# A ninth harmonic in half-height matmuls, and feature rows gathered once and doubled by ScalarE, in a four-layer graph kernel

## The reference

```python
h = jnp.maximum(_layernorm(x, axis=-1), 0.0)
q = (h @ Wq).reshape(n, H, DQK)                       # 8 heads of 16
x_dst = h[edge_dst]                                   # one feature row of 64 for each edge
wk = mlp2(edge_features, k_w1, k_b1, k_w2, k_b2)      # edge weights, 128 each
wv = mlp2(edge_features, v_w1, v_b1, v_w2, v_b2)
# tensor_product: out[e,o] = w[e,o] * sum_{s<9, d<64} x_dst[e,d] * sh[e,s] * C[d,s,o]
k = tensor_product(x_dst, edge_sh, wk, Cqk).reshape(-1, H, DQK)
v = tensor_product(x_dst, edge_sh, wv, Cv).reshape(-1, H, DV)
attn = jnp.einsum('ehd,ehd->eh', q[edge_src], k)
# softmax of attn over the edges of a node, weighted sum of v, W_out, W_self, batch norm
```

## Time and profile before

| | us |
|---|---|
| median of three runs | 3084.54 |
| lowest and highest run | 3083.05, 3087.43 |
| the profiled execution | 3079.32 |
| its span, first to last instruction | 3077.6 |
| TensorE busy in the span | 2460.3 (80%) |
| VectorE busy | 2185.3 (71%) |
| GpSimd busy | 2028.1 (66%) |
| ScalarE busy | 869.0 (28%) |

### The profile page before, as it was taken

How to read it: one execution, slowest core, us unless ns; L and a number is a source line. 1 busy time by engine, 2 the same in 40 slices (tenths; PEclk the granted TensorE clock), 3 DMA queues, 4 the chain that set the end, 5 groups by cost and what they waited for, 6 DMA issues and landing times. The chain is left out here.

```text
span 3077.6 us, 51541 instructions
## 1 busy us (share of the span) xinstructions
PE 2460.3 (80%) x14042; PEld 2123.6 (69%) x14042; DVE 2185.3 (71%) x5057; ACT 869.0 (28%) x2421; POOL 2028.1 (66%) x2116
## 2 busy tenths in 40 slices
PE   6777777525676677477777778999999999999997
PEld 5677777525566566355555557888888888888884
DVE  5555555536888888555555564888888888888885
ACT  1111111136666664111111111222232232222233
POOL 4777777457777771177777746777777766677630
PEclk9777767657888888599999987999999999999996
DMA  3444443133333330145555557898888888899850
GB/s 94 93 88 87 86 86 86 32 69 63 60 59 60 61 56 7 29 154 154 162 154 159 158 153 187 213 215 210 206 207 214 205 208 204 204 214 206 205 136 11
DMA packets 334088, 404.37 MB, mean 131 GB/s; under 512 B 171480, under 2 KB 203334, under 8 KB 333898
## 3 DMA queue, kind: packets, MB, share of 16 engines
q1 hardware_dynamic: 252362, 251.19, 35.2%
q0 software_dynamic: 66560, 96.41, 14.8%
q10 hardware_dynamic: 14976, 54.53, 5.2%
HBM read 339.81 MB, written 62.07 MB: 131 GB/s over the span
## 5 line engine op out<-in xcount | busy, mean ns | idle before, releaser
L1941 PE MATMUL psum<-ckv,z 128*128 128x256 f32 x4160 | 967.1, 383 | 0.0
L1941 PEld LDWEIGHTS psum<-ckv,z 128*128 128x128 f32 x4160 | 766.1, 191 | 97.7
L1776 POOL DMA_INDIRECT acc<-QW,dst_i x416 | 398.5, 958 | 183.9 <-issue 111.5
L234 POOL DMA_INDIRECT ga<-TA,src_i x416 | 411.0, 988 | 155.9 <-issue 126.5
L1786 POOL DMA_INDIRECT ga<-XX,src_i x416 | 399.6, 961 | 156.5 <-issue 122.5
L1033 POOL DMA_INDIRECT ga<-T,src_i x416 | 401.4, 965 | 147.2 <-issue 125.9
L234 POOL DMA_INDIRECT ga<-T,src_i x416 | 396.0, 952 | 149.2 <-issue 124.3
L2058 DVE TENSOR_TENSOR z<-psum,shb 128x2560 f32<-128x2560 f32 x104 | 293.2, 2819 | 58.6 <-PE psum L1932 58.3
L1127 PE MATMUL psum<-HT,wy 128*128 128x128 f32 x1664 | 263.4, 323 | 65.7 <-DVE wy L1400 64.9
L451 PE MATMUL psum<-wre,re 128*128 128x68 f32 x832 | 210.9, 345 | 129.4 <-DVE oneT L296 81.7
L1127 PEld LDWEIGHTS psum<-HT,wy 128*128 128x128 f32 x1664 | 241.5, 231 | 83.7 <-DVE wy L1400 77.1
(11 more groups left out here) (366 smaller groups left out, 4199.0 us busy)
## 6 DMA issues: line engine op xcount, KB each, us to landing
shb<-in_ea SPq DMA_DIRECT2D x104, 640.0 KB, 6.9
WKV<-wkvo ACTq DMA_DIRECT2D x104, 512.0 KB
shb<-in_ea SPq DMA_DIRECT2D x104, 512.0 KB, 9.1
wkv<-WKV SPq DMA_DIRECT2D x104, 512.0 KB
dl<-DL SPq DMA_DIRECT2D x208, 128.0 KB
win<-TB SPq DMA_DIRECT2D x416, 32.0 KB
ga<-T,src_i POOLq DMA_INDIRECT x832
ef<-in_ea SPq DMA_DIRECT2D x104, 128.0 KB
```

The costliest lines, as they stand in the source:

```text
L234: pool.indirect_dma_start(o, None, table, bass.IndirectOffsetOnAxis(ap=src_i[:, g * GT + t:g * GT + t + 1], axis=0)).then_inc(s_g[k], 16)
L1776: pool.indirect_dma_start(qg[:, (g % QR) * GT + t, :], None, QW, bass.IndirectOffsetOnAxis(ap=dst_i[:, g * GT + t:g * GT + t + 1], axis=0) ...
L1941: last = pe.matmul(kv_of(k)[:, t, :], z[:, k % 2, j, t * 128:(t + 1) * 128], ckv[:, j, :], start=(j == 0), stop=(j == NZ - 1))
```

## The change

The table `XX` holds each feature row once (256 bytes), stored straight from the normalised rows `H`; the second copy in the node stage is gone. The gathers fill the first 64 columns of a place in `ga`. A new ScalarE step, `second_halves`, waits for the gather of a group and copies the 64 columns to the other 64; it stands at the head of ScalarE's body and works for the group one ahead, and the transposes wait for it (`e3_two`) instead of the gather.

The ninth harmonic is now loaded into both halves: the lower half is used for tiles 0 and 1, the upper for tiles 2 and 3, by a third transfer of 2 x 128 columns per group. The upper half of the last slot of `ckv` holds the ninth constants too. In front of the first tile's products stand four matmuls with 64 rows of contraction, one per tile, in the order 0, 2, 1, 3, so that lower and upper half alternate; they open the accumulation. Each tile then has four products with 128 rows.

```diff
-        XX = dram("XX", [N, 2 * D])
+        XX = dram("XX", [N, D])
-        NL3 = 9
+        NL3 = 11
-        twice = nodes[:, NJ * D:3 * NJ * D].rearrange("p (j a f) -> p j a f", j=NJ, a=2)
-                pool.memset(ckv[D:128, NZ - 1, :], 0.0).then_inc(n3_p, 1)
-                        pool.indirect_dma_start(ga[:, (g % GR) * GT + t, :], None, XX, bass.IndirectOffsetOnAxis(
+                        pool.indirect_dma_start(ga[:, (g % GR) * GT + t, 0:D], None, XX, bass.IndirectOffsetOnAxis(
...
+                    late = bass.ds(g * GT * W + 2 * W, 2 * W)
+                    sp.dma_start(shb[D:128, k % 2, NZ - 1:NZ, 2 * W:], A["ea9"][NS - 1:NS, late].partition_broadcast(D)).then_inc(e3_e[k % 2], 16)
...
+                    L(m[D:128, NZ - 1:NZ, :], A["L3_gnn_" + w][:, NS - 1:NS, :])
...
-                    sp.wait_ge(n3_x, h + 1)
-                    put_rows(sp, XX.rearrange("(p j) f -> p j f", p=PN)[:, J, :], twice[:, J].rearrange("p j a f -> p j (a f)"), n3_ox)
+                    sp.wait_ge(n3_h, h + 1)
+                    put_rows(sp, XX.rearrange("(p j) f -> p j f", p=PN)[:, J, :], H[:, J, :], n3_ox)
...
+                def second_halves(i, k):
+                    act.wait_ge(e3_g[k], i * 64 + 64)
+                    rows = ga[:, (k % GR) * GT:(k % GR + 1) * GT, :]
+                    act.activation(rows[:, :, D:F], rows[:, :, 0:D], ACT.Copy).then_inc(e3_two, 1)
+
                 def body(i, k):
                     p1, p2 = soft_1(i, k), soft_2(i, k)
+                    n = i * UG + k + 1
+                    if n < NT // GT:
+                        second_halves(n // UG, n % UG)
...
-                for h, (J, _) in enumerate(HALVES):
-                    act.wait_ge(n3_h, h + 1)
-                    act.activation(twice[:, J, 1, :], twice[:, J, 0, :], ACT.Copy).then_inc(n3_x, 1)
...
                 act.wait_ge(e3_i, 3)
+                second_halves(0, 0)
                 each_step(act, body)
...
-                    pe.wait_ge(e3_g[k], i * 64 + 64)
+                    pe.wait_ge(e3_two, g + 1)
...
-                    for j in range(NZ):
+                        for u in (0, 2, 1, 3):
+                            half = slice(0, D) if u < 2 else slice(D, 128)
+                            pe.matmul(kv_of(k)[:, u, :], z[half, k % 2, NZ - 1, u * 128:(u + 1) * 128], ckv[half, NZ - 1, :],
+                                      start=(u % 2 == 0), stop=False, skip_group_check=True)
+                    for j in range(NZ - 1):
                         last = pe.matmul(kv_of(k)[:, t, :], z[:, k % 2, j, t * 128:(t + 1) * 128], ckv[:, j, :],
-                                         start=(j == 0), stop=(j == NZ - 1))
+                                         start=False, stop=(j == NZ - 2), skip_group_check=True)
...
-                dve.memset(shb[D:128, :, NZ - 1, :], 0.0).then_inc(e3_pad, 1)
+                dve.memset(shb[D:128, :, NZ - 1, 0:2 * W], 0.0).then_inc(e3_pad, 1)
...
-                    dve.wait_ge(e3_e[k % 2], i * (UG // 2 * 32) + (k // 2 + 1) * 32)
+                    dve.wait_ge(e3_e[k % 2], i * (UG // 2 * 48) + (k // 2 + 1) * 48)
```

More of the change, by code:

```diff
@@ L1713, in build @@
         NODE3 = len(R3) * 5 + 2
-        e3_zero = sem("e3_zero")
+        e3_zero, e3_two = sem("e3_zero"), sem("e3_two")
         e3_gq = [sem(f"e3_gq{k}") for k in range(UG)]
@@ L1980, in node_transposes @@
                     for j in range(n):
-                        last = pe.transpose(bank[r % 2][0:D, j * PN:(j + 1) * PN], twice[:, j0 + j, 0, :], ident[0:PN, 0:PN])
+                        last = pe.transpose(bank[r % 2][0:D, j * PN:(j + 1) * PN], H[:, j0 + j, :], ident[0:PN, 0:PN])
                     last.then_inc(n3_t, 1)
@@ L2007, in _ @@
                 pe.wait_ge(n3_qc, len(R3))
-                pe.wait_ge(n3_p, 1)
                 pe.sem_inc(e3_S, SPARE)
@@ L2040, in _ @@
                 for J, _ in HALVES:
-                    dve.scalar_tensor_tensor(twice[:, J, 0, :], XC[:, J, :], 0.0, st[:, 5, J].unsqueeze(2).to_broadcast([PN, J.stop - J.start, D]),
+                    dve.scalar_tensor_tensor(H[:, J, :], XC[:, J, :], 0.0, st[:, 5, J].unsqueeze(2).to_broadcast([PN, J.stop - J.start, D]),
                                              ALU.max, ALU.mult).then_inc(n3_h, 1)
```

## The result

The changed kernel takes 3068.06 us, the median of 8 runs (3061.38 to 3072.81). The kernel before, run beside it, takes 3083.90 us (8 runs, 3077.94 to 3087.43). The ratio is 0.9945, with a 95% interval of 0.9935 to 0.9955: 0.55% faster. Forecast were 3063 us and a range of 3048 to 3098.

A forecast was written before the change was run, and what follows sets the result against it. TensorE and VectorE were both near their limit, with VectorE's chain the bound afterwards. 28 us gained in groups 11 to 103 less 7 lost at the start gave net -21, 3058 us against the profile, 3063 as median; range 3048 to 3098.

The forecast's parts named there:

- loss at the start: Bodies 6 and 10 of the fourth edge stage: ScalarE waits for a gather ahead of dT; +7.5 us once, bounds +2 and +10.
- overlap of the half products: Front of each group's products: 64-row matmuls on different halves run beside each other, saving three slots, 0.65 us per group.
- change between full and half rows: TensorE, going in and out of the half-row products: 0.2 us charged per group, bounds 0 to 0.29.
- TensorE's net saving: TensorE in each group, products saved less the price of changing row height: 0.45 us.
- TensorE's own work: TensorE's time without waits over a cycle of four groups: 42.73 us before, 40.93 us after the change.
- VectorE's chain: VectorE's own dependent steps over four groups, without waits for TensorE: 41.97 us, unchanged, and setting the period afterwards.
- gain, groups 11 to 103: Steady part of the fourth edge stage: 93 groups at 0.30 us each, 28 us gained.
- before the first transposes: Node stage to first gathers: fewer ScalarE copies and a halved table save 0 to 2 us, a copy costs 0.42; -0.5 taken.
- Who is late next: Steady part: VectorE's 41.97 us stand above TensorE's 40.93 per four groups; VectorE's waits for TensorE go, 0.30 us per group.
- ScalarE's waits for gathers: ScalarE after 2100 us: such waits would show that gathers gate, a rival at 3070 to 3088 us, chance 0.10.
- DMA: DMA engines: shorter gather rows save 0.43 us per group, the new 64 KB cost about 0.3; share up 0.02 or 0.03.
- No overlap: Rival, front of each group's products: 64-row matmuls don't overlap, TensorE is the bound at 43.53 us per cycle; 3098 us, chance 0.19.

## Why the prediction was right, point by point

The sign, the mechanism and the range held; the time is 5 us above the forecast. Two terms of the sum were mis-sized, in opposite directions: the gain was put 8 us too high, the loss at the start 1.4 to 2.7 us too high. That they partly cancel is luck.

| step | predicted | measured |
|---|---|---|
| overlap of the half products, per group | 0.65 us | 0.86 us |
| change between full and half rows | 0.20 us | 0.38 us |
| TensorE's net saving, per plain body | 0.45 us | 0.48 us |
| TensorE's own work, one cycle | 40.93 us | 40.86 us |
| VectorE's chain, one cycle | 41.97 us | 42.21 us, mean 42.32 |
| gain, groups 11 to 103 | 28 us | 19.66 us |
| loss at the start | 7.5 us | 4.83 us at group 11, 6.08 at 15 |
| before the first transposes | -0.5 us | -0.26 us |
| sum | -21 us | -15 us |

**The products.** Two errors cancel, by luck. Four slots are saved, not three: my picture of passes that begin in issue order is wrong. The change of tiling costs 0.09 us ahead of the half products (0.53 us after the transposes start, where full rows followed at 0.44), 1.06 - 4 x 0.216 = 0.20 us with them, and 0.10 us in the eight full products behind (1.83 us to the sums, 8 x 0.216 = 1.73), 0.39 us by this count. I took its price from a single one-row transpose, and the upper bound of 0.29 was too low. The page "TensorEngine Tiling (Array Packing)" of the Trainium skill (Key Properties) says that a change of mode drains TensorE. The trace shows that the change costs time, 0.38 us for both directions; whether it is a drain it doesn't show, since the ends of matmuls in it are modelled.

**Who is late next.** Right, and the experiment without the ninth harmonic shows it, though the cycle of 42.2 to 42.3 us lies above the 41.9 to 42.1 that I had named as the sign. The size of the gain is the step that failed: I put it at all that VectorE waited for TensorE, 1.22 us per cycle. The measured gain is 43.30 - 42.32 = 0.98 us, and the difference of 0.24 is the wait of z for prow. In before this wait is not on the list: z waited 0.49 us for the transposes at the same place, and a wait is put down to what came last. By the order of the program the second one lay under it, half as long. Removing a wait uncovers the next at the same instruction; the chain I worked out without TensorE's waits had to be put together from what each step needs, not by subtraction. Over 92 groups 0.06 us make 5.5 of the 8.3 us. Most of the rest is a wait in body 14 (below).

**The start.** The place and the mechanism are right: gather 7 holds ScalarE, dT comes behind it, and VectorE and TensorE stand. The size was 7.5 at group 11, and came out at 4.83. I had said that by body 14 the lead is large enough. It isn't: at 2028.88 VectorE waits another 2.12 us for dT, and between groups 11 and 15 the loss grows to 6.08 us.

**ScalarE's waits for gathers.** I had named them, after 2100 us, as the sign that gathers gate. They are there: 39.7 us from 2100 to 2900, up to 5.7 us at a time, and harmless, since ScalarE is idle then and nothing behind the wait is late. The sign that tells is VectorE's wait for dT, which is missing after body 14.

**DMA.** I had the new 64 KB at 0.3 us of all 16 engines per group, and a rise of the share by 0.02 or 0.03. It rose by 0.05. With and without that transfer the share is 0.97 and 0.92 at the same cycle of 10.6 us, so it takes 0.5 us. The shorter gather rows give about as much back (0.85 against 0.89 of 10.8 us, 0.43 us, as predicted). I called both zero for the time. For TensorE and VectorE they are; but with 512-byte rows the half products alone scatter up to 3103 us. What the shorter rows are worth is room on the DMA engines, and that I did not see.

**The rivals.** No overlap was put at 3098 us and measures 3124. Its condition was right, its price was not: against before it was put at +14 us and is +35 (3123.62 against 3088.51 beside it). TensorE's own work with overlap is 2 x 9.93 + 10.53 + 10.47 = 40.86 us per cycle. (The first softmax body lasts 11.54 us, and in it L681 starts 1.44 us after the transposes, where in before it was 0.43: 1.01 us are waiting.) Eight slots instead of four add 4 x 0.86 = 3.4, 44.3 in all, where I had 43.53, mostly because the change of tiling costs 0.38 us and not 0.2. The measured 44.65 holds another 0.36 us of waiting for VectorE: L681 starts 0.79 us after the transposes there (2515.58 and 2516.37). The bound from which no overlap would decide, a net saving of 0.16 us per group, doesn't follow from the prediction's own figures either: (42.73 - 41.97) / 4 is 0.19.

## What to carry to other kernels

A list of waits names for each instruction only the one that came last, so a gain that is read from it is an upper bound: look for what the same instruction needs next, and when that is ready. When two engines are within 3% of each other, find out which chain is the bound by taking work from each in turn; here 75 us in 800 less of TensorE's work gave nothing, and two small copies taken from VectorE gave 12 us (3062.62 to 3050.68). A new wait on an idle engine that works in order belongs behind whatever another engine is waiting for, and ahead of anything that itself waits late: against before, the same copy of 0.4 us cost 6 us of the start at the head of the body and 2 us behind dT; at the body's end the kernel got 120 us slower than after, part of it by the lower clock that followed the stall.

## What the runs showed of the hardware

- Two float32 matmuls of 64 rows on different halves start together and follow in pairs every 0.216 us, the pace of one full-row instruction, whether they are issued alternating or one half after the other. On one half they follow one by one at the same pace.
- Going from full rows to 64-row products and back cost 0.38 us in a plain body, spread over three places, and not as a gap at one of them.
- After TensorE had stood 3.6 us in every cycle, its granted clock was 0.51 for 7 us; the body behind took 12.40 us, the next one 9.94.
- A transfer of 64 KB took 0.5 us of 16 engines, about 0.05 of their time, where its share of the bytes is 0.03. With the DMA share at 0.94 the runs agree within 11 us; at 0.97 they scatter over 44 us; at 1.03 transfers are late and the time is 1.0% above before (0.4 to 1.6%).
